# A mixture-of-experts feed-forward computed token by token, with the gate as a per-row scalar

## What is computed

```python
x = x + 0.5 * ffn(layernorm(x))
x = x + attention(layernorm(x))      # 16 query heads, 4 key heads, 128 wide, causal, rotary
x = x + 0.5 * ffn(layernorm(x))

def ffn(z):                          # z: tokens x 256, E = 8 experts, 2 of them count
    logits = z @ router_w + router_b
    vals, idx = top_k(logits, 2)
    full_w = sum(one_hot(idx, E) * softmax(vals)[..., None])      # tokens x E
    h = einsum('td,edf->etf', z, expert_w) + expert_b[:, None, :]
    combined = einsum('etf,te->tf', silu(h), full_w)
    y = z + combined @ proj_w + proj_b
    return norm_w * y / sqrt(mean(y * y) + 1e-6)
```

## Time and profile before

| | |
|---|---|
| median of 3 runs | 891.71 us (891.23 to 893.34) |
| profiled execution, first to last instruction | 890.8 us |
| busy, share of that span | TensorE 92%, VectorE 79%, POOL 66%, ScalarE 59% |
| mean granted clock of TensorE | 0.971 of full speed |
| first feed-forward | 0 to 170.9 us |
| attention | 170.9 to 743.5 us |
| second feed-forward | 743.5 to 890.8 us |

### The profile page before, as it was taken

One profiled execution on the slowest core, in us unless ns is written; L12 is line 12 of the kernel. 1 busy time (PEld: TensorE's weight loads), 2 busy tenths in 40 slices (PEclk: granted clock), 3 DMA queues, 4 the chain that ended last, 5 costly groups with the idle time before them and its releaser, 6 DMA issues. The chain is left out here.

```text
span 890.8 us, 17017 instructions
## 1 busy us (share of the span) xinstructions
PE 822.6 (92%) x4848; PEld 724.0 (81%) x4848; DVE 701.0 (79%) x1824; ACT 521.4 (59%) x1252; POOL 585.2 (66%) x444
## 2 busy tenths in 40 slices
PE   5998888767999999999999999999999998999984
PEld 4776776656889999999999899899999986787873
DVE  6899989899776776776866867767767797789987
ACT  3654534445765765755865766756767663554542
POOL 3667746368587687777777787777777812556743
PEclk9999988978999999999999999999999999899998
DMA  8053153410212311312312312212212100000001
GB/s 302 1 178 105 72 201 142 142 36 12 49 24 59 106 24 35 94 35 59 94 24 47 94 24 71 85 33 47 71 41 54 25 1 29 1 1 24 24 1 47
DMA packets 26673, 55.98 MB, mean 63 GB/s; under 512 B 3568, under 2 KB 9840, under 8 KB 25104
## 3 DMA queue, kind: packets, MB, share of 16 engines
q1 hardware_dynamic: 26640, 55.59, 21.4%
HBM read 22.02 MB, written 12.58 MB: 39 GB/s over the span
## 5 line engine op out<-in xcount | busy, mean ns | idle before, releaser
L1050 POOL TENSOR_TENSOR at_ql<-at_rot,at_qh 128x512 fp32r<-128x512 f32 x62 | 79.8, 1287 | 99.6 <-ACT at_qh L1272 99.6
L1289 ACT ACTIVATE at_pr<-at_sm,at_low 128x512 f32<-128x512 f32 (+3 forms) x256 | 140.4, 555 | 0.9 <-DVE at_low L1137 0.8
L1295 ACT ACTIVATE at_pth<-at_pt 128x512 fp32r<-128x512 f32 (+1 forms) x192 | 95.8, 525 | 76.0 <-PE at_pt L1449 75.2
L603 ACT ACTIVATE f_s<-f_ex,f_cols 128x512 f32<-128x512 f32 x128 | 84.1, 686 | 86.0 <-PE f_ex L751 46.3
L293 POOL TENSOR_TENSOR f_acc<-f_acc,f_u 128x512 f32<-128x512 f32 x68 | 100.8, 1509 | 40.8 <-DVE f_u L482 27.7
L1147 DVE TENSOR_SCALAR at_pr<-at_pr,at_inv 128x128 f32<-128x128 f32 (+3 forms) x256 | 113.1, 504 | 2.3
L1137 DVE CUSTOM_DVE_ANT_0 at_sm<-at_sc,at_mask 128x512 f32<-128x512 f32 (+3 forms) x256 | 109.8, 484 | 2.5 <-issue 2.4
L1152 DVE TENSOR_TENSOR at_ptl<-at_pt,at_pth 128x512 fp32r<-128x512 f32 (+1 forms) x192 | 108.7, 593 | 1.7 <-ACT at_pth L1295 1.5
L1059 POOL TENSOR_TENSOR at_rot<-ga,cos 128x512 f32<-128x512 f32 x78 | 104.2, 1336 | 4.1 <-POOL at_ql L1050 2.4
L1065 POOL TENSOR_TENSOR at_rot<-at_rot,gc 128x512 f32<-128x512 f32 x78 | 101.5, 1301 | 8.1 <-POOLq L1082 2.1
L1449 PE MATMUL at_pt<-ident,at_pr 128*128 128x128 f32 x640 | 96.3, 278 | 9.3 <-DVE at_pr L1147 6.8
(11 more groups left out here) (212 smaller groups left out, 2262.7 us busy)
## 6 DMA issues: line engine op xcount, KB each, us to landing
gc<-ga SPq DMA_DIRECT2D x160, 128.0 KB, 2.3
ga<-in_attn_w SPq DMA_DIRECT2D x4, 1280.0 KB, 7.7
attn_split<-gb SPq DMA_DIRECT2D x4, 1280.0 KB, 9.6
attn_split<-gc SPq DMA_DIRECT2D x4, 1280.0 KB, 12.1
gb<-attn_split SPq DMA_DIRECT2D x8, 512.0 KB, 4.2
at_wo<-attn_split SPq DMA_DIRECT2D x8, 512.0 KB, 4.3
x<-in_x SPq DMA_DIRECT2D x4, 512.0 KB, 9.0
e_raw<-in_expert_w SPq DMA_DIRECT2D x8, 256.0 KB, 6.7
```

The lines of the kernel that those rows point to most:

```text
L1289: act.activation(pr[h % 2][:, cols], sm[h % 2][:, cols], ACT.Exp, bias=low[h % 2][:, i:i + 1], scale=-1.0, accum_out=tot[h % 2][:, i:i + 1 ...
```

## The change

`ffn_phase` is turned round: tokens lie on the partitions. z is stationary, 128 tokens at a time, and the weights of two experts move, 2 x 256 columns. A unit is one tile of 128 tokens and one pair of experts: six matmuls into one bank, 16 units a block, in two halves `g` of two tiles each. SiLU is applied in place in PSUM. The gate is now one number per partition, so VectorE takes it as a scalar: `weighted` does, for each expert of the unit, one operation of 256 columns that multiplies and adds to `acc`. `weights_T`, `select`, `pick`, the rings and the sums on POOL and VectorE are gone.

A per-feature bias can't be a per-partition bias any more. It goes into the weights: zh holds z + 1, and from the weights a column's sum, less the bias, over 256 is taken away, so that the ones bring the bias in. For that the first phase sums the weights with fp32 matmuls against a matrix of ones (`sum_weights`), ScalarE turns the sums into shifts, and VectorE (pair 0) and POOL (pairs 1 to 3, `shift_pair`) add them to `e_raw`. The router's offset `r_off` is made likewise. `acc` has tokens on its partitions and is transposed for the projection (`sum_T`), half a block at a time.

`group_rest` moves from VectorE to POOL, and groups stand at the half blocks 1, 3, 5 and 6 (`GROUP_AT`): group 3 in the first half of block 3. The loops are written out. The second feed-forward finds the first pair of experts split by the end of attention (`first_pair`) instead of the first expert.

The diff, cut to its core:

```diff
-        SUMS = (1, 2, 3, 5, 7)
...
-            def select(i, e, prev):
-                if e == 0:
-                    pe.wait_ge(wT_done, i + 1)
-                if e < 2 and prev:
-                    pe.wait_ge(yadd_done, 2 * (i - 1) + e + 1)
-                if e >= 2:
-                    pe.wait_ge(mult_done, MULT0 + C * E * i + C * (e - 1))
-                pe.matmul(w_ps[e % 2][:], pick[:, e, :], wT[:], start=True, stop=True).then_inc(sel_done, 1)
...
+        GROUP_AT = {1: 0, 3: 1, 5: 2, 6: 3} if first else {}
...
+            def store_group(k):
+                sp.wait_ge(a_lo_done, 2 * k + 2)
+                if k + 1 < KV:
+                    load_group(k + 1)
+                sp.dma_start(split[k, 0], a_hi[:].bitcast(F32)).then_inc(a_out, 16)
+                sp.dma_start(split[k, 1], a_lo[:].bitcast(F32)).then_inc(a_out, 16)
...
+            def shift_pair(p):
+                pool.wait_ge(shift_done, p)
+                w = e_raw[:, 2 * p:2 * p + 2, :].rearrange("p e (c d) -> p e c d", c=C)
+                pool.tensor_tensor(w, w, shift[:, p - 1].unsqueeze(2).to_broadcast([P, 2, C, D]), ALU.add).then_inc(e_shifted, 1)
...
+            def group_rest(k, half):
+                part = slice(half * GW // 2, (half + 1) * GW // 2)
+                pool.wait_ge(a_hi_done, 2 * k + half + 1)
+                pool.tensor_tensor(a_lo[:, part], a_raw[:, part], a_hi[:, part].bitcast(F32), ALU.subtract).then_inc(a_lo_done, 1)
...
+            def body(i):
+                group = GROUP_AT.get(2 * i)
+                if group is not None:
+                    scale_queries(group)
+                if i > 0:
+                    inverse_rms(i - 1, 1)
+                if i < LAST:
+                    residual(i + 1)
+                if i > 0:
+                    add_rows(i - 1, 1)
+                if group is not None:
+                    group_rest(group, 0)
+                    group_rest(group, 1)
+                group = GROUP_AT.get(2 * i + 1)
+                if group is not None:
+                    scale_queries(group)
+                    group_rest(group, 0)
+                inverse_rms(i, 0)
+                if i + 2 < NORMS:
+                    rstd(i + 2)
+                add_rows(i, 0)
+                if group is not None:
+                    group_rest(group, 1)
...
+            def shift_first():
+                dve.wait_ge(sum_ready, 1)
+                for c in range(C):
+                    w = e_raw[:, 0:2, c * D:(c + 1) * D]
+                    dve.scalar_tensor_tensor(out=w, in0=ex_ps[0][:].rearrange("p (e d) -> p e d", e=2), scalar=-1.0 / D, in1=w,
+                                             op0=ALU.mult, op1=ALU.add).then_inc(first_shifted, 1)
...
+            def weighted(i, g, p):
+                full_w = full[:, i % 2]
+                if p == 0 and g == 0:
+                    dve.wait_ge(gate, GATE * (i + 1))
+                if p == 0 and i > 0:
+                    dve.wait_ge(ct_done, 2 * (i - 1) + g + 1)
+                for half in range(2):
+                    e = 2 * p + half
+                    for t in range(HT):
+                        n, tile = unit(g, p, t), HT * g + t
+                        h = ex_ps[n % RING][:, half * D:(half + 1) * D]
+                        if half == 0:
+                            dve.wait_ge(silu_done, UNITS * i + n + 1)
+                        if e == 0:
+                            dve.tensor_scalar(acc[:, tile, :], h, full_w[:, tile, e:e + 1], None, ALU.mult).then_inc(acc_done, 1)
+                        else:
+                            dve.wait_ge(acc_done, SUMS * i + 4 * (PAIRS * g + p) + HT * half + t - HT + 1)
+                            dve.scalar_tensor_tensor(out=acc[:, tile, :], in0=h, scalar=full_w[:, tile, e:e + 1],
+                                                     in1=acc[:, tile, :], op0=ALU.mult, op1=ALU.add).then_inc(acc_done, 1)
...
+            def sum_rest(i, g):
+                dve.wait_ge(chi_done, 2 * i + g + 1)
+                dve.tensor_tensor(cl[:, g], w_ps[1 - g][:].rearrange("p (c k) -> p c k", c=C), ch[:, g].bitcast(F32),
+                                  ALU.subtract).then_inc(clo_done, 1)
...
+            def body(i):
+                weighted(i, 0, 0)
+                if i > 0:
+                    sum_rest(i - 1, 1)
+                if i + 1 < NORMS:
+                    norm_rows(i + 1)
...
+                weighted(i, 0, 2)
+                if i > 0:
+                    mean_square(i - 1, 1)
+                weighted(i, 0, 3)
+                if i > 0:
+                    scale_rows(i - 1, 1)
+                if i + 1 < NORMS:
+                    z_rest(i + 1)
+                if i == 0:
+                    dve.wait_ge(p_hi_done, 1)
+                    dve.tensor_tensor(p_lo[:], p_raw, p_hi[:].bitcast(F32), ALU.subtract).then_inc(p_split, 1)
+                weighted(i, 1, 0)
+                sum_rest(i, 0)
+                weighted(i, 1, 1)
+                add_residual(i, 0)
+                weighted(i, 1, 2)
+                mean_square(i, 0)
+                if i < LAST:
+                    choose(i + 1)
+                weighted(i, 1, 3)
+                scale_rows(i, 0)
+                if i < LAST:
+                    weigh_chosen(i + 1)
+                if i + 2 < NORMS:
+                    norm_stats(i + 2)
...
+            def silu(i, g, p, t):
+                n = unit(g, p, t)
+                act.wait_ge(ex_done, UNITS * i + n + 1)
+                act.activation(ex_ps[n % RING][:], ex_ps[n % RING][:], ACT.Silu).then_inc(silu_done, 1)
...
+            def body(i):
+                silu(i, 0, 0, 0)
+                silu(i, 0, 0, 1)
+                if i == 0:
+                    pair_lead(2)
+                if i > 0:
+                    sum_lead(i - 1, 1)
+                silu(i, 0, 1, 0)
+                silu(i, 0, 1, 1)
+                if i == 0:
+                    pair_lead(3)
+                group = GROUP_AT.get(2 * i)
+                if group is not None:
+                    group_lead(group, 0)
+                silu(i, 0, 2, 0)
+                if i > 0:
+                    squares(i - 1, 1)
+                silu(i, 0, 2, 1)
...
+            def sum_weights(p):
+                pe.wait_ge(e_in[p], 32)
+                o = ex_ps[p][:].rearrange("p (e d) -> p e d", e=2)
+                for c in range(C):
+                    pe.matmul(o, ones[:], e_raw[:, 2 * p:2 * p + 2, c * D:(c + 1) * D], start=(c == 0), stop=False)
+                pe.matmul(ex_ps[p][:], e_row[:, 0:P], e_row[:, P + 2 * p * D:P + 2 * (p + 1) * D], start=False, stop=True).then_inc(sum_ready, 1)
...
+            def sum_T(i, g):
+                pe.wait_ge(acc_done, SUMS * i + SUMS // 2 * (g + 1))
+                if g == 1:
+                    pe.wait_ge(xn_done, BT * i + HT)
+                elif i > 0:
+                    pe.wait_ge(xn_done, BT * i)
+                for c in range(C):
+                    for t in range(HT):
+                        r = pe.transpose(w_ps[1 - g][:, (HT * c + t) * P:(HT * c + t + 1) * P],
+                                         acc[:, HT * g + t, c * P:(c + 1) * P], ident[:])
+                r.then_inc(ct_done, 1)
...
+            def body(i):
+                experts(i, 0, 0)
+                if i > 0:
+                    sum_T(i - 1, 1)
+                experts(i, 0, 1)
+                if i > 0:
+                    project(i - 1, 1)
+                experts(i, 0, 2)
+                if i + 1 < NORMS:
                     transpose_z(i + 1)
+                experts(i, 0, 3)
+                experts(i, 1, 0)
+                sum_T(i, 0)
+                if i < LAST:
+                    router(i + 1)
+                experts(i, 1, 1)
+                project(i, 0)
+                experts(i, 1, 2)
+                if i < LAST:
+                    logits_back(i + 1)
+                experts(i, 1, 3)
```

839 lines of the change are left out of this document (335 added, 504 removed).

## The result

The changed kernel takes 907.3 us (median of four runs, 905.4 to 907.9), the kernel before 891.5 (890.9 to 893.3): ratio 1.0173, 95% interval 1.0156 to 1.0189.

The account below looks back on a forecast made before the run. Neither engine's work sets a block (TensorE 27.4 us, VectorE about 25); their order does. First FFN +15.9, attention +0.5, second FFN -5.7 on the 890.8 us span give 901.5; plus 0.9 is 902.4, stated as 902.5, range 889 to 915.

Parts of the forecast that it names:

- the head: First FFN up to block 0's last expert matmul: new fp32 weight sums delay it to 52.3 us from 43.3, +9.0.
- the second FFN: Block 0 ends at 780.5, block 2 at 845.1, the whole at 885.1 us against 890.8: -5.7.
- the tail of the first FFN: From the end of block 2 to the first FFN's end: 69.9 us where the old kernel took 58.5, +11.4.
- attention: Middle phase, hardly edited: first_pair splits two experts instead of one at its end, +0.5 us.
- Steady blocks: Blocks 1 and 2 of each FFN: 32.3 us each, from 27.4 of TensorE work and 4.7 of waits.
- VectorE's walk: One block's operations followed in order from the previous block's last expert matmul, giving TensorE's waits; VectorE work about 25 us.
- The half-clock rival: Idles drop TensorE to 1.2 GHz in the steady blocks, up to 10 us more: 912 us; chance 0.2.
- The PSUM rival: Multiply-adds take their full 0.48 us, 1.3 us a block, 9 over seven blocks: 911 us; chance 0.05.
- The errata figure: A PSUM source costs VectorE 62 cycles more, 0.065 us an operation; the prediction found the trace against it.
- Block 3: First FFN: ACT waits from 7 to 25.7 us for stores, TensorE restarts at 30.2, wb allows step 2 at 54.3.
- the last rival: No group wait: stores land sooner or ACT's order matters less, block 3 loses 13 us of stall, 889.5 us; chance 0.1.
- First FFN together: Whole first FFN: +9.0 to block 0's end, -4.5 for blocks 1 and 2, +11.4 from there on, sum +15.9 us.

Follow-up runs that it names:

- e2: Changed kernel with every weight group in the first half of its block (half blocks 0, 2, 4, 6); 897.3 us, ratio 1.0068 to the kernel before.
- e7: Changed kernel with SiLU written to a ring of four SBUF tiles that weighted reads instead of PSUM; 920.2 us, ratio 1.0316 to the kernel before.
- e9: Changed kernel with only the head reordered: norm 1 statistics and gate earlier, two row scalings behind the gate; 907.7 us, ratio 1.0155 to the kernel before.
- e1: Changed kernel with weight group 3 moved from the first to the second half of block 3; 907.2 us, ratio 1.0173 to the kernel before.
- e3: Changed kernel with norm_stats moved from the block's end to behind sum_rest in its second half; 910.0 us, ratio 1.0204 to the kernel before.
- e5: e3 with weigh_chosen put ahead of scale_rows instead of behind it; 904.7 us, ratio 1.0136 to the kernel before.
- e6: e2 and e5 together on the changed kernel; 892.1 us, ratio 1.0027 to the kernel before.
- e8: Changed kernel with a pair's weights laid out contiguously, except the second FFN's first pair; 906.9 us, ratio 1.0172 to the kernel before.
- e10: e6 and e9 together, with POOL's group remainders ahead of add_rows and group 0 scaled behind the residual; 878.1 us, ratio 0.9855 to the kernel before.
- e11: Changed kernel with group_rest back on VectorE in the same half blocks; 905.5 us, ratio 1.0180 to the kernel before.
- e12: e10 with scale_rows ahead of the gate again and POOL's first-half add_rows behind the next block's root; 882.3 us, ratio 0.9927 to the kernel before.

## Why the prediction was right, and where its terms were not

The direction and the size held: 902.5 forecast, 907.3 measured, inside 889 to 915. Some of that is luck: on the profiled span the head was worse by 6.9 us and the second FFN by 2.9, and the tail of the first FFN (2.8) and attention (4.4) made up for most of it. By its own steps:

**Steady blocks**: 32.3 us forecast, 32.05 measured; blocks 1 and 2 together 64.6 and 64.1. The waits were at the forecast places, but smaller: `project` 1.5 us idle for 2.2, `router` 0.5 for 1.3, `sum_T` 0.1 to 0.2 for 1.2; all idle time of a block is 2.5 us for 4.7. The work was larger: the 512-column step is 0.233 us, not 0.228, which gives 28 us rather than 27.4, and refilling after transposes takes 0.3 to 0.8 us that the sum of steps left out. Two errors of about 2 us cancelled (and the forecast's 27.4 and 4.7 make 32.1, not 32.3). VectorE's walk assumed four `norm_rows` at their plain price; they took 4 us beside POOL, and e2 prices that at 0.6 us a block.

**The half-clock rival** fell: the granted clock of the steady blocks is 1.00.

**The PSUM rival** fell: line 435 takes 477 ns, the forecast's 478, and in a row of four the starts lie 0.40 us apart (91.91, 92.31, 92.70, 93.09), not 0.48; e7, with both sources in SBUF, has the same. Only the four plain multiplies of a block were mis-sized, 0.40 apart for 0.33. The errata figure of the Trainium skill that the prediction weighed ("VectorE: DVE Perf Modes", section on the TRN2 errata), a higher fixed cost for PSUM sources, isn't seen on the multiply-adds; its advice on small tiles is, since 256 columns cost 0.40 apart and 512 cost 0.60.

**The head** was mis-sized: block 0 ends at 59.2, not 52.3. Two terms are at fault. The fp32 matmul was taken at 0.40 us. A pair's three, two over the weights (line 714, in four instructions, shown) and one over the bias row (line 715), take 2.86 us from start to start:

```profile
12.48 1.88 PE L714 MATMUL f_ex<-e_raw,f_ones 128*128 128x512 f32 x4
...
16.83 1.88 PE L714 MATMUL f_ex<-e_raw,f_ones 128*128 128x512 f32 x4
```

(12.48 to 15.34, and 16.83 to 19.69), 0.95 each on average, 4.2 times 0.228; the two over the weights take 0.91. The four passes of a true fp32 matmul that the Trainium skill states in "FP8 and Floating Point Precision" (TensorE Precision Notes), and which the prediction priced at 2.7 us and left out of the sum, are borne out. The first three, at half of that speed, took 4.5 us (7.05 to 11.54) for the forecast's 2.6. The second term wasn't there at all, POOL beside VectorE:

```profile
18.44 3.35 POOL L251 TENSOR_TENSOR f_zres<-z,f_rows 128x1024 f32<-128x1024 f32 x1
...
19.57 2.25 DVE L525 TENSOR_SCALAR f_rows<-f_rows 128x16 f32<-128x16 f32 x1
...
21.85 2.41 DVE L527 TENSOR_SCALAR f_rows<-f_rows 128x256 f32<-128x256 f32 x1
...
21.75 2.36 POOL L258 TENSOR_TENSOR e_raw<-e_raw,f_shift 128x1024 f32<-128x1024 f32 x1
```

Scaling 128 x 16 numbers takes 2.25 us and 128 x 256 takes 2.41, each ending with POOL's instruction; with the splits stretched from 1.21 to 2.54 us the same way, `weighted` began at 30.1 instead of 26.4. The other 3.2 us lie in block 0 itself, 29.1 us instead of 26, where TensorE stands 7.0 us for the split of pair 2 (35.87); e9 shortens that wait to 2.5 us, and its head is 4.8 shorter.

**Block 3.** The chain was forecast step by step, most of it within 2 us: remainder at 12.8 us into the block (11.3), stores landed at 25.7 (24.7), ACT idle from 7 to 25.7 (17.4 us), TensorE restarts at 30.2 (28.6), `wb` at 54.3 (54.2), the FFN ends at 69.9 (67.1). The match of `wb` is luck: the last remainder ended 3.3 us earlier than forecast (38.9 for 42.2), and stores and load took 15.3 us instead of 11.8. The sum for the stores has a slip too (12.8 and 12.1 make 24.9, not 25.7). What was wrong is what the stand was held to cost: the last rival took 13 us off for it (889.5), and e1, without the stand, took 907.2. Issue of the last stores, end of the FFN and TensorE's wait for `wb`, in us:

| | store issued | FFN ends | between | wait for `wb` |
|---|---|---|---|---|
| before | 145.1 | 170.9 | 25.8 | none |
| changed | 162.2 | 190.4 | 28.2 | 6.5 |
| e1 | 163.6 | 190.3 | 26.7 | 19.5 |
| e2 | 154.5 | 181.8 | 27.3 | 7.1 |
| e3 | 170.1 | 199.2 | 29.1 | 6.6 |
| e5 | 157.0 | 186.7 | 29.7 | 6.8 |
| e6 | 151.2 | 179.2 | 28.0 | 7.0 |
| e7 | 175.5 | 200.4 | 24.9 | none |
| e8 | 166.4 | 194.6 | 28.2 | 6.4 |
| e9 | 161.7 | 190.9 | 29.2 | 7.1 |
| e10 | 137.4 | 161.7 | 24.3 | 0.9 |
| e11 | 162.6 | 187.1 | 24.5 | none |
| e12 | 147.9 | 173.0 | 25.1 | 2.7 |

Where TensorE waits 2.7 us or more for `wb`, the end follows that store: 25 to 30 us behind it, over a range of 22 us of the store. In the kernel before, in e7 and in e11 it doesn't wait, and something else sets the end; the like distance there says nothing of the chain.

**First FFN together**: +15.9 forecast, +19.5 measured: the head is 6.9 us worse, the blocks 0.5 better, the tail 2.8 better.

**Second FFN**: -5.7 forecast, -2.8 measured. Block 0 came 1.4 us late (38.4 us for 37.0), blocks 1 and 2 1.7 early (62.9 for 64.6), block 3 and the tail 3.2 late (43.2 for 40.0): TensorE's mean granted clock was 0.88 from 849.20 on, and it stood idle for 2.9 us ahead of the last `sum_T` and 1.4 behind it.

**Attention**: +0.5 forecast, -3.9 in the profiled execution. This is probably not the change's. e1 has the same attention code, and from the phase's first matmul (190.29, and 190.56 in the changed kernel) to the second FFN's first `router` (767.01 and 762.34) it took 576.7 us and the changed kernel 571.8; the kernel before took 575.9. The two part 20 us into the phase, at the first transposes of probabilities. The changed kernel, TensorE and then VectorE:

```profile
210.54 1.10 PE L1426 MATMUL at_pt<-ident,at_pr 128*128 128x128 f32 x8 [3.10 <-DVE at_pr L1122]
...
215.38 1.27 DVE L1122 TENSOR_SCALAR at_pr<-at_pr,at_inv 128x128 f32<-128x128 f32 x4
```

and e1:

```profile
210.27 1.97 PE L1426 MATMUL at_pt<-ident,at_pr 128*128 128x128 f32 x8 [4.40 <-DVE at_pr L1122]
...
215.82 2.32 DVE L1122 TENSOR_SCALAR at_pr<-at_pr,at_inv 128x128 f32<-128x128 f32 x4
```

TensorE's eight transposes took 1.10 us in one and 1.97 in the other, VectorE came to the divisions behind them 0.7 us later (counted from the phase's first matmul), met POOL there and took 2.32 us for 1.27, and the order of collisions differs from then on. In the thirteen profiled executions with this code the same distance is 571.4 to 573.2 us in eight and 576.2 to 576.9 in five. So most or all of the -3.9 is probably chance of one execution, which may also be why the medians differ by more than the spans; each kernel was profiled once, so that one kernel shows both lengths isn't seen. Over those transposes TensorE's granted clock was 0.86 in the changed kernel (210.5 to 212.0) and 0.50 in e1 (210.2 to 212.2). That this starts the difference is read from these rows; it wasn't forced by an experiment.

## What to carry to other kernels

Ask for each VectorE operation whether POOL runs beside it and whether it is a `tensor_scalar` or a two-source operation wholly in SBUF; if so, its size may not count and POOL's does. Then give small operations a PSUM source, or a place where POOL is waiting. And before moving a stand-still, follow the chain that it waits for to its end: here moving the stand alone gained nothing (e1), and what shortened block 3 and its tail by 13 and 22 us was where the groups and the last remainder stand (e2, e10). A change that lets an engine start earlier (e3) is to be read for what it will then run beside.

## What the runs showed of the hardware that wasn't expected

- A `tensor_scalar` of 4 elements a partition took 1.27 us and a product of 32 took 2.81, each ending with the POOL instruction beside it (e3). Between e3 and e5 the blocks differ by 4 to 6 us.
- A true fp32 matmul of 512 columns takes 0.95 us on average; each shows as two instructions.
- The head has two speeds. In e2's execution the four instructions of a pair's fp32 sums take twice as long as at 12.48 above:

```profile
14.76 3.62 PE L714 MATMUL f_ex<-e_raw,f_ones 128*128 128x512 f32 x4
```

while the granted clock reads 1.00 in that stretch in both. Of the twelve profiled executions with these sums, four had the quicker head and eight the other. Block 0 ends about 4 us later for it (`logits_back` at 56.1, or at 60.2 in e8, whose sums ran at half speed). Why the clock column doesn't show it, and what decides it, stays open. With attention's two lengths it would explain why one kernel's runs spread over 8 us or more (e2, e6, e9); only one execution of each is profiled, so this isn't shown.
- SiLU from PSUM to PSUM without a bias takes 583 ns; from PSUM to SBUF with a bias per partition it was 686, and without one 600 (e7).
